# Decoder megakernel, prologue: GpSimd decodes three of the eight packed weight pieces and VectorE five, instead of two and six

## The reference

```python
NVFP4_LUT = jnp.array([0.0, 0.5, 1.0, 1.5, 2.0, 3.0, 4.0, 6.0,
                       0.0, -0.5, -1.0, -1.5, -2.0, -3.0, -4.0, -6.0], dtype=jnp.float32)
low = W_packed & 15
high = W_packed >> 4 & 15
idx = jnp.stack([low, high], axis=-1).reshape(N, -1)
vals = NVFP4_LUT[idx]
vals = vals.reshape(N, K // block, block) * scales[:, :, None]
...
gate = jnp.einsum('th,nh->tn', xt, Wg)
up = jnp.einsum('th,nh->tn', xt, Wu)
inter = gelu * up
out = jnp.einsum('tn,hn->th', inter, Wd)
```

## Time and profile before

| | us |
|---|---|
| time, median of 3 runs (2198.62 to 2200.77) | 2199.52 |
| span of the profiled execution, first to last instruction | 2203.6 |
| prologue, up to the loop's first DMA issue | 192.75 |
| DVE busy in the prologue | 176.05 |
| GpSimd busy in the prologue | 93.46 |

### The profile page before, as it was taken

The page is one execution under the profiler, slowest core; times in us unless marked ns, Lnnn a source line. Parts: engine busy times, 40 slices in busy tenths (PEclk is TensorE's granted clock), DMA queues, the critical chain, the costliest instruction groups (busy, mean ns, idle before and its releaser), DMA issues. The chain is left out here.

```text
span 2203.6 us, 27072 instructions
## 1 busy us (share of the span) xinstructions
PE 1636.9 (74%) x10018; PEld 959.6 (44%) x10018; DVE 1438.5 (65%) x3114; ACT 737.8 (33%) x1187; POOL 294.7 (13%) x365
## 2 busy tenths in 40 slices
PE   5021777599898777776796667589998868875888
PEld 3021554322254654554454445422255644553644
DVE  8997664688645665677543764678744674676643
ACT  1020331299722301341311331089922401331310
POOL 7900120000000221022000120000000230221100
PEclk9555887799999898987898887779999889987989
DMA  3024000000021101000023000000012011000012
GB/s 139 14 84 153 1 1 15 22 1 1 3 65 50 58 11 52 32 1 1 1 72 119 1 1 15 22 0 1 1 46 72 1 58 62 1 32 1 1 44 67
DMA packets 23348, 73.01 MB, mean 33 GB/s; under 512 B 2224, under 2 KB 6704, under 8 KB 21168
## 3 DMA queue, kind: packets, MB, share of 16 engines
q1 hardware_dynamic: 19152, 61.30, 8.3%
q10 hardware_dynamic: 4064, 9.96, 1.3%
HBM read 63.91 MB, written 7.34 MB: 32 GB/s over the span
## 5 line engine op out<-in xcount | busy, mean ns | idle before, releaser
L938 PE MATMUL PS<-acts,ring 128*128 128x512 f32 (+1 forms) x624 | 287.4, 606 | 4.5 <-ACT acts L1189 2.7
L1336 POOL TENSOR_TENSOR rstd<-rstd,half_neg 128x4 f32<-128x4 f32 x30 | 30.3, 1008 | 1431.8 <-DVE rstd L1423 1300.4
L780 PE MATMUL PS<-const,acts 128*128 128x128 f32 x256 | 60.2, 400 | 214.7 <-DVE acts L1425 75.8
L1189 ACT COPY acts<-PS 128x512 f32<-128x512 f32 x84 | 49.3, 587 | 466.1 <-PE PS L780 466.0
L1268 ACT ACTIVATE scratch<-PS,log 128x512 int16<-128x512 f32 x256 | 196.2, 956 | 4.5 <-PE PS L1043 4.5
L1677 DVE TENSOR_REDUCE XNM<-PS 128x1 f32<-128x1024 f32 x128 | 156.6, 1223 | 40.7 <-PE PS L1029 39.3
L1260 ACT ACTIVATE scratch<-PS,XNM 128x1024 bf16<-128x1024 f32 x128 | 175.9, 1374 | 10.0 <-DVE XNM L1677 9.7
L938 PEld LDWEIGHTS PS<-acts,ring 128*128 128x128 f32 (+1 forms) x624 | 118.9, 192 | 131.6 <-issue 121.7
L804 PE MATMUL PS<-arena,acts 128*128 128x256 f32 (+2 forms) x512 | 173.2, 498 | 2.5 <-DVE tmp L1864 2.1
L1204 ACT COPY QTX<-PS 96x1024 bf16<-96x1024 bf16 x96 | 92.2, 1011 | 211.8 <-PE PS L825 211.8
L847 PE MATMUL PS<-QTX 96*128 96x128 bf16 x1536 | 152.2, 233 | 10.4 <-DVE QTX L1485 10.4
(11 more groups left out here) (349 smaller groups left out, 3033.7 us busy)
## 6 DMA issues: line engine op xcount, KB each, us to landing
ring<-in_f SPq DMA_DIRECT2D x46, 384.0 KB, 3.0
ring<-f_weights SPq DMA_DIRECT2D x32, 384.0 KB, 3.0
f_weights<-scratch ACTq DMA_DIRECT2D x12, 384.0 KB, 2.8
QTX<-in_toeplitz SPq DMA_DIRECT2D x2, 2048.0 KB, 8.2
arena<-in_pk_l3f SPq DMA_DIRECT2D x2, 1673.0 KB, 7.4
arena<-in_pk_l2a SPq DMA_DIRECT2D x2, 1152.0 KB, 5.1
arena<-in_pk_l0f SPq DMA_DIRECT2D x2, 1056.0 KB, 8.0
arena<-in_pk_l1a SPq DMA_DIRECT2D x2, 1056.0 KB, 10.0
```

The source lines that it names most:

```text
L780: mm = pe.transpose(PS[:, g // 2, at:at + P], src(g, c), ident)
L938: mm = pe.matmul(PS[0:m, F_UP[i % 2][u]], w[:, u * E + c * P:u * E + c * P + m], src[:, c], start=c == 0, stop=c == EC - 1)
```

## The change

One number of a pair moves. Piece 2 is no longer DVE's first but GpSimd's third, and DVE decodes pieces 3 to 7.

```diff
-POOL_PIECES, DVE_PIECES = 2, 6
+POOL_PIECES, DVE_PIECES = 3, 5
```

## The result

| | before, us | after, us |
|---|---|---|
| time, median of 4 runs each | 2199.07 (2198.02 to 2200.77) | 2228.31 (2226.38 to 2231.56) |
| ratio | | 1.0128, 95% interval 1.0114 to 1.0142 |
| span of the profiled execution | 2203.6 | 2229.7 |
| prologue, up to the loop's first load | 192.75 | 218.65 |
| rest of the span (the loop) | 2010.85 | 2011.05 |

The changed kernel is slower by 1.28%. In the profiled executions the whole difference lies ahead of the loop: 218.65 - 192.75 = 25.9 us, and 0.2 us behind it.

The account below looks back on a forecast made before the run. The prediction took VectorE to bound the prologue, whose end moves the whole loop. A decode saved, -8.4 us, and VectorE's loss beside GpSimd's third piece, +33.5 us, gave +25.1 us, 2224.6 us, range 2217 to 2232 us (its own 2220 to 2229).

Parts of the forecast that it names:

- Bounds: End of the prologue: VectorE's last decode holds the barrier, so each microsecond it shifts moves the whole loop by one.
- The gain: VectorE's decodes in the prologue: one piece fewer saves 8.4 us, wholly on the path.
- The start of the third piece, and its DMAs: GpSimd in the prologue: third piece runs from about 111.0 to 154.7 us, and its DMAs cost nothing.
- The loss: VectorE's key splits beside GpSimd's third piece: the engines take turns, which costs VectorE 33.5 us.
- The walk through the instructions: Key splits from 111.0 us: VectorE does twelve, ten and six instructions, reaching the eighth split at 154.7 us, 33.7 us late.
- The sum: Whole kernel: -8.4 + 33.5 = +25.1 us, giving 2224.6 us on the median.
- The faster one: Rival, 111 to 155 us: split works as busy times suggest, 2191.1 us without loss, faster below 8.4 us loss; chance 5%.
- Whole blocking by all 19 instructions: Rival, third piece: every GpSimd instruction holds VectorE back, +28.5 us, 2228.0 us; chance 8%.
- the later third piece: Rival: third piece starts or runs 5 to 15 us later and meets reduction L633, +20.7 us, 2220.2 us; chance 7%.
- GpSimd did not become the bound: Rival, prologue: GpSimd becomes the bound, for which it would have to end after 210 us; chance under 1%.

Follow-up runs that it names:

- skip_piece: Kernel before, with VectorE decoding five pieces, GpSimd still two, and the eighth piece filled by a second store of the first's result: 2196.17 us, ratio 0.9975.
- pool_one: Kernel before, with GpSimd decoding one piece and VectorE seven: 2178.91 us, ratio 0.9887.
- third_unstored: Kernel before, VectorE keeping its six pieces, with GpSimd also loading and decoding a third piece whose result is not stored: 2234.43 us, ratio 1.0148.
- pool_none: Kernel before, with GpSimd decoding no piece and VectorE all eight: 2163.37 us, ratio 0.9825.
- third_late: Changed kernel, with GpSimd's third piece waiting for the end of VectorE's quantised values (L641): 2225.28 us, ratio 1.0113 against the kernel before.
- form_l386: Kernel before, with 15 unused GpSimd instructions of L386's form (float32 in, bfloat16 out) added behind its second piece: 2220.81 us, one execution.

## Why the prediction was right

**Bounds.** The prologue's end hung on VectorE as said. Every shift of VectorE's last decode came out at the loop's first load: 8.37, 34.3, 25.9 us.

**The gain.** -8.4 us stated, 8.37 us in skip_piece's profile. Its medians alone would say 5.6 us.

**The start of the third piece, and its DMAs.** Stated 111.0 to 154.7 us, found 111.18 to 155.0 us. The loads cost nothing.

**The loss.** Stated 33.5 us, found 34.4 us in the changed kernel and 34.3 us where it stood alone. The price of the second piece, from which it was taken, was 33.3 us stated and 33.8 us by pool_one. The walk through the instructions came out: VectorE finished eleven beside L384 to L387, ten beside L388 to L404 and seven from there to GpSimd's end, 28 in all, where twelve, ten and six were stated. The first of them, L320 of the fourth split, was already running when the piece began, so the eighth split had not begun at GpSimd's end as the walk has it. It began just behind, at 155.12 us, and 155.12 - 120.72 = 34.4 us is the whole delay.

**The sum.** 25.1 us stated, 25.9 us by the profiles. The medians say 29.2 us and, the second time, 27.6 us, with intervals that together reach from 1.0106 to 1.0142, or 23 to 31 us. 25.1 us lies at the very end of the first interval, and the 2224.6 us that were forecast are 3.7 us below the measured median, inside the range of 2220 to 2229 us. The 1.7 to 3.3 us by which the medians stand above the profiles were found in no row. The loop differs by more than that from one execution to another. Over the other comparisons too the medians shift by something else than the profiled prologues, and not always by more: +2.8 us in skip_piece, -1.6 us in third_unstored, 0 in pool_one, -0.3 us in pool_none, -0.6 us in third_late. That fits chance and does not prove it. This stays open.

**The rivals.** The faster one fell: the loss was four times its turning point of 8.4 us. Whole blocking by all 19 instructions fell as a mechanism, since L324 took 0.29 us beside L386 again, although 2228.0 us happens to be nearest to the measured median. The premise of the later third piece, that the reduction L633 passes beside GpSimd, is borne out: form_l386's took its 4.42 us. Its price was not tested, because third_late begins the piece 26.5 us later than the changed kernel, past the reduction and beside the decodes, where the profile shows 0.9 us less loss and not 4.4 us less. GpSimd did not become the bound: it ended at 155.0 us.

## What to carry to other kernels

Idle time of GpSimd is not free capacity for a busy VectorE. Before moving elementwise work from VectorE to GpSimd, look at VectorE's rows beside GpSimd's: if short ones swell and end together with GpSimd's, price the move by GpSimd's time less what VectorE gets done in its turns, and not by the instructions moved. How much that leaves depends on the instructions of both: a decode cost VectorE 34.4 us of its 43.8 us beside short instructions, and 20.3 us of its 51.5 us beside long ones. Here one piece saved 8.4 us and cost 20 to 34 us, and the best split was to give GpSimd none.

## What the runs showed of the hardware

- VectorE's casts, copies and instructions with two SBUF inputs were held beside most of GpSimd's instructions, and the two engines took turns. A held instruction ends sooner behind the release than its own length: L340, 0.23 us alone, ended 0.08 us behind GpSimd's L389, and L349, which the prediction has running for 1.08 us behind L402, takes 1.23 us in pool_none. So part of it is done while it waits. GpSimd is held too: its third piece lasts 43.8 us beside the key splits, and 48.1 us beside VectorE's decodes in third_late.
- Some VectorE instructions were not held at all. Three rows of the kernel before lie wholly inside GpSimd's L400 or L401 and are as long as in pool_none, where GpSimd is idle: L599 with one input in PSUM (2.29 us in both), the reduction L344 (2.29 us in both) and the reciprocal L346 (0.95 us in both). L348 behind them, with two SBUF inputs, took 5.21 us in place of 2.29 us. GpSimd first, then VectorE:

```profile
37.77 6.23 POOL L400 TENSOR_SCALAR tmp<-acts 128x1536 bf16<-128x1536 bf16 x1
44.09 5.40 POOL L401 TENSOR_SCALAR acts<-acts 128x1536 bf16<-128x1536 bf16 x1
```

```profile
38.80 2.29 DVE L599 TENSOR_TENSOR scratch<-PS,arena 128x2048 f32<-128x2048 f32 x1
41.12 2.29 DVE L344 TENSOR_REDUCE small<-scratch 128x128 f32<-128x2048 f32 x1
...
44.12 0.95 DVE L346 RECIPROCAL small<-small 128x128 f32<-128x128 f32 x1
45.11 5.21 DVE L348 TENSOR_TENSOR scratch<-scratch,small 128x2048 f32<-128x2048 f32 x1
```

- How long a GpSimd instruction blocks depends on its form. L386's form (44.67 us for fifteen) blocked a single VectorE instruction for at most some 0.65 us at a time (L320, 0.94 us in place of 0.29 us), and let several through between. L389's form (43.59 us for eight) blocked a cast or a copy to its end (5.50 us for L320). An instruction with two SBUF inputs was over some 1.0 us before the end of such a GpSimd instruction: in the changed kernel L323 ended at 140.09 us and GpSimd's L401 at 141.12 us. That reading and writing are held apart would explain it, and is only argued.
- The Trainium skill ("SBUF — State Buffer", "Who interferes with whom") has the loser blocked for the whole instruction, and reductions exempt. These traces agree on the reductions and on casts beside L389's form. They differ on L386's form and on the two-input instructions, and the measurement decides.
- The loop of one and the same program took 2003.5 to 2011.6 us in single executions, and the stretch up to L618, beside the same GpSimd piece, 67.1 to 67.4 us or 69.7 to 70.3 us. No run shows what decides between the two.
